# Two more dense groups, a reordered opening and VectorE operands in PSUM in a two-layer graph network kernel on Trainium2

## The reference

```python
edge_index = jnp.stack([src, dst])
deg = jnp.maximum(segment_sum(ones, dst), 1.0); deg_isqrt = deg ** (-0.5)
h = jnp.maximum(_layernorm(x), 0.0)
# layer 0: one of two linear maps per edge, by its type, summed at dst
msg = where(type == 0, h[src] @ W_data.T + b_data, h[src] @ W_control.T + b_control)
x = x + relu(segment_sum(msg, dst) + h @ W_self.T + b_self)
h = jnp.maximum(_layernorm(x), 0.0)
# layer 1: gated sum
g = tanh((h @ gw[:128])[dst] + (h @ gw[128:])[src] + gb)
yn = tanh(ew * yes_w + (1 - ew) * no_w)
e = (g + yn) * 0.5 * deg_isqrt[dst] * deg_isqrt[src]
x = x + segment_sum(h[src] * e[:, None], dst)
```

## Time and profile before

| | us |
|---|---|
| median of 3 runs | 5841.05 (5840.38 to 5857.13) |
| the profiled execution, its own time | 5829.9 |
| its span, first to last instruction | 5828.1 |

### The profile page before, as it was taken

One profiled execution on the slowest core, in us unless ns is written; L12 is line 12 of the kernel. 1 busy time (PEld: TensorE's weight loads), 2 busy tenths in 40 slices (PEclk: granted clock), 3 DMA queues, 4 the chain that ended last, 5 costly groups with the idle time before them and its releaser, 6 DMA issues.

```text
span 5828.1 us, 119944 instructions
## 1 busy us (share of the span) xinstructions
PE 4286.3 (74%) x29542; PEld 3197.4 (55%) x29542; DVE 4365.5 (75%) x16525; ACT 3038.4 (52%) x10494; POOL 4307.3 (74%) x4285
## 2 busy tenths in 40 slices
PE   6588888888888888875577777777777777777754
PEld 5355666655565555553455555555555555555543
DVE  7887777878787777755467777777777777777863
ACT  5666666666666666643254544544445444444530
POOL 5777777777777777777457777777777777777774
PEclk8599999999999999987688888888888888888875
DMA  7777777777777777776355455555555455455544
GB/s 239 245 217 223 222 224 223 225 221 223 225 225 224 223 223 222 220 224 203 102 134 121 118 118 119 121 119 120 119 119 121 119 119 119 118 120 118 120 97 116
DMA packets 764988, 979.91 MB, mean 168 GB/s; under 512 B 135667, under 2 KB 567063, under 8 KB 763799
## 3 DMA queue, kind: packets, MB, share of 16 engines
q1 hardware_dynamic: 620131, 687.26, 40.0%
q0 software_dynamic: 135168, 281.42, 19.7%
q10 hardware_dynamic: 9012, 3.56, 0.2%
HBM read 911.05 MB, written 60.67 MB: 167 GB/s over the span
## 4 chain that ended last, share of the span: by engine, by line
POOL 72%; issue 23%; PE 2%; DVE 2%; DMA 1%; SPq 1%; ACTq 0%; DVEq 0%; POOLq 0%; ACT 0%
POOL G L570 72%; SPq L311 1%; PE PS L883 0%; DMA OWF<-in_x 0%; DMA out<-OWF 0%; DVE ST L1172 0%; DVE OHF L1183 0%; DVE G L1639 0%; PE PS L891 0%; DMA G<-t,IDXB 0%; PE PS L1054 0%; PE PS L1057 0%; DVE OWF L1191 0%; DVE OWF L1832 0%; PE PS L1081 0%
## 5 line engine op out<-in xcount | busy, mean ns | idle before, releaser
L570 POOL DMA_INDIRECT G<-t,IDX x4016 | 4019.1, 1001 | 1274.3 <-issue 1223.0
L1081 PE MATMUL PS<-CDST,HTB 128*128 128x256 f32 x2352 | 868.3, 455 | 447.7 <-DVE CDST L1768 419.9
L705 ACT ACTIVATE OHF<-PS 128x384 bf16<-128x384 f32 x1764 | 864.6, 490 | 515.7 <-PE PS L927 488.0
L939 PE MATMUL PS<-CDST,OHF 128*128 128x256 bf16 x5292 | 901.0, 281 | 35.0 <-DVE ACC L1283 35.0
L797 ACT ACTIVATE ST<-PS,MV 128x1 f32<-128x1 f32 x1764 | 457.5, 259 | 720.2 <-issue 327.6
L1072 PE MATMUL PS<-HTB,OWF 128*128 128x129 f32 x3528 | 815.1, 317 | 9.7 <-DVE OWF L1747 9.7
L1072 PEld LDWEIGHTS PS<-HTB,OWF 128*128 128x128 f32 x3528 | 720.5, 218 | 166.8 <-issue 75.9
L1081 PEld LDWEIGHTS PS<-CDST,HTB 128*128 128x128 f32 x2352 | 408.0, 217 | 556.0 <-ACT HTB L816 510.4
L939 PEld LDWEIGHTS PS<-CDST,OHF 128*128 128x128 bf16 x5292 | 532.6, 101 | 315.8 <-issue 68.7
L1081 PE MATMUL PS<-OHF,OWF 128*128 128x256 f32 x1176 | 438.6, 459 | 246.5 <-DVE OHF L1768 230.2
L1300 DVE TENSOR_SCALAR CDST<-IO,BASE 128x256 bf16<-128x256 int16 x1764 | 510.8, 305 | 5.0 <-PE PS L939 4.1
(11 more groups left out here) (240 smaller groups left out, 8316.9 us busy)
## 6 DMA issues: line engine op xcount, KB each, us to landing
HTB<-t0s SPq DMA_DIRECT2D x442, 384.0 KB
OWF<-t0s SPq DMA_DIRECT2D x440, 384.0 KB
HTB<-t SPq DMA_DIRECT2D x882, 132.0 KB
G<-t,IDX POOLq DMA_INDIRECT x4016
YN<-rows SPq DMA_DIRECT2D x882, 64.0 KB
OHF<-rows SPq DMA_DIRECT2D x882, 64.0 KB
t0s<-HTB SPq DMA_DIRECT2D x25, 384.0 KB
t0s<-OWF SPq DMA_DIRECT2D x24, 384.0 KB
```

Of the source, the lines that this page charges most:

```text
L570: eng.indirect_dma_start(out=G[:, k:k + width], out_offset=None, in_=table, in_offset=bass.IndirectOffsetOnAxis(ap=at, axis=0)).then_inc(s ...
L705: eng.activation(X0[:, k % KX, :, :].rearrange("p n w -> p (n w)"), PS[:, cell_bank(k), 0:384], ACT.Identity).then_inc(q_ev, 1)
L939: ins = eng.matmul(PS[:, 4, 0:DW], X0[:, k % KX, n, :], CD0[:, k % KD, :], start=b == 0 and n == 0, stop=b == NB - 1 and n == 2)
L1081: eng.matmul(PS[:, 4 + g % 2, 0:DW], X1[k % KX1], CD1[k // 2 % 3][:, k % 2, :], start=b == 0, stop=b == NB - 1).then_inc(d_ap, 1)
```

## The change

- RUNS becomes 20 groups of 62 tiles: DT = 1240 dense tiles, 1880 gathers per layer, SM = 235 steps, 1960 cells per layer.
- The opening runs TensorE's `turn` and `messages` in halves of a chunk (4 and 3 blocks), keeps the Relu's result in ACC, forms the self part after all messages, and stores ini after t0. `scales` reads the mean from PSUM (MP). src is loaded before dst, typ earlier; `windows` follows the rows.
- `pair_hots` becomes `quad_hots`: one-hots of four cells (QC) in one operation, with a ring of RT = 6 chunks and three quads. A new tensor NX of 12 KB per partition holds them; dynamic_dma_scratch_size is 4096 for the default.
- The counts OHS are formed by one tensor_reduce in place of two additions.
- In layer 1 the number row IOP and the one-hot OHP lie in PSUM bank 5; the group sum has bank 4 alone; `hot1` and `targets1` move behind `weight1`; target hots are made one pair ahead in five buffers; group_add1 moves into the cell loop.

The diff, cut (TensorE's, ScalarE's and SP's waits follow the renamed semaphores):

```diff
-RUNS = ((16, 62), (2, 60))
+HALF = ((0, 4), (4, CB))
+RUNS = ((20, 62),)
...
-RT = 4
+RU = 4
+RT = 6
+QC = 4
...
-KD1, KX1, KW1 = 6, 6, 8
+KD1, KX1, KW1 = 5, 6, 8
...
+        NX = sb("NX", [128, 3072])
+        HT0 = blocks(ACC[:, 0, 0:NB * 128])
+        MP = PS[:, 2, 0:NB]
+        IOP = PS[:, 5, 0:DW]
+        OHP = PS[:, 5, DW:DW + TG * W].rearrange("p (j w) -> p j w", w=W)
...
             for c in range(NC):
-                if c == 4:
+                if c == 2:
                     eng.wait_ge(s_stg, 1)
                     load(STI, typ, s_typ)
-                eng.wait_ge(a_ye, c + 1)
-                chunk_dma(eng, YB[c % 2], t0, c, False, a_t0[c % 2])
-                if c >= 1:
-                    eng.wait_ge(a_se, c)
-                    eng.dma_start(ini[:, (c - 1) * CB * 128:c * CB * 128],
-                                  ACC[:, 0, (c - 1) * CB * 128:c * CB * 128]).then_inc(s_ini, 16)
...
+                for first, last in HALF:
+                    table_half(c, first, last)
             eng.wait_ge(s_zr, 17)
             for c in (NC - 2, NC - 1):
-                eng.wait_ge(a_t0[c % 2], landed(c, 2))
+                eng.wait_ge(a_t0[c % 2], stored(c))
+            for c in range(NC):
+                eng.wait_ge(a_se, c + 1)
+                eng.dma_start(ini[:, c * CB * 128:(c + 1) * CB * 128],
+                              ACC[:, 0, c * CB * 128:(c + 1) * CB * 128]).then_inc(s_ini, 16)
...
             turn(0)
+            turn(1)
+            for h in range(2 * NC):
+                messages(h)
+                if h + 2 < 2 * NC:
+                    turn(h + 2)
             for c in range(NC):
-                if c + 1 < NC:
-                    turn(c + 1)
...
+                    ins = eng.matmul(PS[:, c % 2 * 2 + n, 0:CB * 64], WS[:, :], ACC[:, 0, at:at + CB * 64],
+                                     start=True, stop=True)
...
                 eng.wait_ge(a_sq, c + 1)
+                eng.tensor_copy(MP[:, cols].unsqueeze(2), MV[:, cols, 0:1])
                 link(eng.reciprocal(RS[:, cols], SQ[:, cols]))
-                eng.scalar_tensor_tensor(DG[:, cols].unsqueeze(2), MV[:, cols, 0:1], -1.0, RS[:, cols].unsqueeze(2),
+                eng.scalar_tensor_tensor(DG[:, cols], MP[:, cols], -1.0, RS[:, cols],
                                          ALU.mult, ALU.mult).then_inc(a_rs, 1)
...
-                eng.wait_ge(m_oh, 2 * n - 1)
-                if n >= 2:
-                    eng.wait_ge(m_os, n - 1)
-                quads = OH[:, b, :, :].rearrange("p (q j) w -> p q j w", j=QT)
-                eng.tensor_tensor(OHT[:, :, :, :], quads[:, :, 0:2, :], quads[:, :, 2:4, :], ALU.add).then_inc(m_oh, 1)
-                eng.wait_ge(m_oh, 2 * n)
-                eng.tensor_tensor(OHS[:, b, :, :], OHT[:, :, 0, :], OHT[:, :, 1, :], ALU.add).then_inc(m_os, 1)
+                eng.wait_ge(m_oh, n)
+                    eng.tensor_reduce(OHS[:, b, :, :], OH[:, b, :, :].rearrange("p (q j) w -> p q w j", j=QT),
+                                      mybir.AxisListType.X, ALU.add).then_inc(m_os, 1)
...
-            def pair_hots(c):
-                eng.wait_ge(q_tc[c % RT], parts_in(c))
-                if c >= 3:
-                    eng.wait_ge(q_ga, HB * (c - 2))
+            def quad_hots(u):
+                for c in (2 * u, 2 * u + 1):
+                    eng.wait_ge(q_tc[c % RT], parts_in(c))
+                if u >= 3:
+                    eng.wait_ge(q_ga, QC * (u - 2))
                 for t in range(2):
-                    ins = eng.tensor_scalar(OT0[c % 3][:, t, :], RB0[:, c % RT, :], PCODE[:, t:t + 1], None,
+                    ins = eng.tensor_scalar(OT0[:, u % 3, t, :], RB0Q[:, u % 3, :], PCODE[:, t:t + 1], None,
                                             ALU.is_equal)
                 ins.then_inc(q_ot, 1)
...
-                        if k % HB == 0 and k + HB < NG * NB:
-                            pair_hots(k // HB + 1)
+                        if k % QC == 0 and k + QC < NG * NB:
+                            quad_hots(k // QC + 1)
...
-                    OH[:, s % 2, :, :], LOC[:, t:t + TG].unsqueeze(2).broadcast_to([128, TG, W]),
-                    IOTA[:, 0:W].unsqueeze(1).broadcast_to([128, TG, W]), ALU.is_equal).then_inc(e_dd, 1)
+                    OHP, LOC[:, t:t + TG].unsqueeze(2).broadcast_to([128, TG, W]),
+                    IOP[:, 0:W].unsqueeze(1).broadcast_to([128, TG, W]), ALU.is_equal).then_inc(e_dd, 1)
...
-                eng.scalar_tensor_tensor(JUNK[k % 2], IO16[:, 0:DW], TABS[:, g % 2, NB + b:NB + b + 1],
+                eng.scalar_tensor_tensor(JUNK[k % 2], IOP, TABS[:, g % 2, NB + b:NB + b + 1],
...
-                if c >= 3:
-                    eng.wait_ge(d_ap, 2 * (c - 2))
-                eng.tensor_tensor(CD1[c % 3], IO16[:, 0:DW].unsqueeze(1).broadcast_to([128, 2, DW]),
+                if c >= KD1:
+                    eng.wait_ge(d_ap, 2 * (c - KD1 + 1))
+                eng.tensor_tensor(CD1[c % KD1], IOP.unsqueeze(1).broadcast_to([128, 2, DW]),
...
+                        if k == (done + 1) * NB + LATE1:
+                            group_add1(done, s - 1)
+                            done += 1
                     if i == 1:
                         score1(s)
-                    if i == 2 and s + 1 < SM:
-                        hot1(s + 1)
-                    if i == 3 and s + 1 < SM:
-                        targets1(s + 1)
                     if i == 4:
                         weight1(s)
+                        if s + 1 < SM:
+                            hot1(s + 1)
+                    if i == 5 and s + 1 < SM:
+                        targets1(s + 1)
```

More of the change, by code:

```diff
@@ L645, in normal, with positive @@
                 ins.then_inc(a_n, 1)
+            def positive(c):
+                for n, (first, last) in enumerate(HALF):
+                    eng.wait_ge(o_t, 2 * c + n + 1)
+                    eng.activation(HT0[:, c * CB + first:c * CB + last, :], strip(0)[:, first:last, :], ACT.Relu)\
+                       .then_inc(o_h, 1)
             eng.wait_ge(s_c, 4)
@@ L650, in _ @@
             normal(0)
-            eng.wait_ge(s_w, 16 * 9)
-            for c in range(NC + 1):
+            root(2, 0)
+            positive(0)
+            normal(1)
+            for c in range(1, NC):
                 if c + 2 < NC:
@@ L1187, in rows @@
             def rows(c):
-                eng.wait_ge(a_m, c + 1)
-                if c >= 2:
-                    eng.wait_ge(a_t0[c % 2], landed(c - 2, 2))
-                eng.tensor_tensor(YB[c % 2], strip(4, 256),
-                                  BB[:, :].unsqueeze(1).broadcast_to([128, CB, 256]), ALU.add)\
-                   .then_inc(a_ye, 1)
+                for n, (first, last) in enumerate(HALF):
+                    eng.wait_ge(o_m, 2 * c + n + 1)
+                    if c >= 2 and n == 0:
+                        eng.wait_ge(a_t0[c % 2], stored(c - 2))
+                    eng.tensor_tensor(YB[c % 2][:, first:last, :], strip(4, 256)[:, first:last, :],
+                                      BB[:, :].unsqueeze(1).broadcast_to([128, last - first, 256]), ALU.add)\
+                       .then_inc(o_y, 1)
             def scales(c):
@@ L1782, in group_add1 @@
                 eng.wait_ge(d_ap, (g + 1) * NB)
[L1783 removed]
+                eng.wait_ge(m_ib, 2 * (SM + NCT + items))
                 if g >= 1:
[L1785 removed]
+                    eng.wait_ge(q_z, NG + g)
                 to = ACC[:, 0, bass.ds(at, DW)]
[L1787 to L1790 removed]
+                eng.tensor_tensor(to, to, PS[:, 4, 0:DW], ALU.add).then_inc(q_z, 1)
+            link(eng.tensor_copy(IOP, IO16[:, 0:DW]))
+            quad_hots1(0)
             for k in range(3):
                 target_score(k)
+            target_hots1(0)
             hot1(0)
@@ L1797, in _ @@
                 ncell = CELL1[s + 1] - CELL1[s]
-                for i in range(max(ncell, 5)):
+                for i in range(max(ncell, 6)):
                     k = CELL1[s] + i
```

287 lines of the change are left out of this document (144 added, 143 removed).

## The result

The changed kernel takes 5397.49 us (median of 4 runs, 5388.35 to 5411.43), the kernel before 5842.56 beside it: a ratio of 0.924, 95% interval 0.922 to 0.926, 445 us less. The forecast was 5400. The lines of the kernel moved: the gathers are L590 (L570 before), the hots of layer 0 L1322 (L1290), TensorE's strips and counts L933 and L939 (L900 and L906), its cells L961 and L973 (L927 and L939), its tiles L992 (L958), the counts L1288 (L1258 and L1260), VectorE's one-hots of the rows, gate and one-hots of the targets in layer 1 L1780, L1794 and L1802 (L1747, L1760 and L1768).

What follows compares the result with a forecast made beforehand. GpSimd's gather after gather was taken as the bound. 97+2413+35+262+2358+22+200 = 5387 us of span, 5389 with the 1.8 outside it, 5400 since the profiled execution lay 11 us below the median; range 5345 to 5560.

Steps and rivals of the forecast that it cites:

- Fewer gathers, same pace in layer 0: Layer 0 main loop: 1880 gathers for 2008 at the old pace of 1.284 us, 2413 us in all.
- A faster gather in layer 1: Layer 1 main loop: operands in PSUM stop VectorE lengthening gathers; pace 1.255 us for 1.328, 2358 us.
- The 22 us for the one bank of the group sum: Layer 1: TensorE waits for group_add1 at 20 groups, a guessed 1 us each, with the edges +22 us.
- Rival D: Layer 1: PSUM operands slow VectorE to 10.7 us a step, 2515 us for 2380, total 5535 us; chance 0.09.
- The terms of VectorE in layer 0: VectorE's need per layer-0 step, from cells, items, tiles and adds: 8.7+1.1 = 9.8 us against GpSimd's 10.27.
- The surcharge of layer 0: Layer 0: 35 us added because GpSimd, VectorE and TensorE are all over 95% taken; nothing given to the six-slot chunk ring.
- engines over 95% taken stall each other in turn: Layer 0 engines: named as what would above all make the forecast fail; no separate size.
- rival E: Layer 0: quad_hots waits for two chunks at once, some 6.0 us a quad, total 6110 us, slower; chance 0.03.
- B: Layer 0: the cells become the bound, 10.9 us a step, +123 for the 35, total 5490 us; chance 0.21.
- the forecast's own signs of being right: Gaps 0.30, gather means 0.95 and 0.98, first gather near 97, GpSimd under 60 us waiting for TensorE, VectorE some 90% busy.
- Opening: Before the first gather: ini stored later, mean read from PSUM; first gather at 97 us, -27.
- Middle and tail: Sections and table between the layers, 262 us, and last sections and output, 200 us: both to stay.

Runs made afterwards that it cites:

- the two runs on the operands: Changed kernel with VectorE's layer-1 operands back in SBUF, 5559.83 us; kernel before with only those operands in PSUM (and what that needs), 5684.39 us.
- the fastest run: Changed kernel with 21 dense groups for 20 and the quad hots of layer 0 made two cells later: 5235.52 us, 0.896 of before.
- the three runs: Changed kernel with hots two cells later, 21 groups and pairs, or pairs and four slots: 8260.97, 8351.38, 8341.87 us where the kernel before took 7871.57.

## Why the prediction was right, point by point

*Fewer gathers, same pace in layer 0.* 1879 intervals at 1.284 were forecast as 2413 us; without the idle places they measure 2412.5.

*A faster gather in layer 1.* Pace 1.255 forecast, 1.261 measured, gather 0.956 for "0.95"; the 0.012 above the 0.944 of an idle VectorE is nearly all L1780, an operation with one tensor input, which the forecast's list of operations with two didn't take in. The cause was argued from one gather of 1.31 us beside L1768 and from the sections' 0.947; the two runs on the operands now show it in both directions, each worth some 160 us. The Trainium skill (SBUF — State Buffer, section "SBUF: two separate sides") says that a VectorE operation with two inputs in SBUF locks the ports that it shares with GpSimd against a GpSimd operation that reads SBUF; the trace agrees (1.048 and 0.956 us with nothing but the operands changed; the gather reads its indices from IDX in SBUF). The 22 us for the one bank of the group sum were too many. From 2900 to 5200 us TensorE's waits show

```profile
PE PS L1116 <- DVE ACC L1821: 82.5, 19, 5.1
```

4.3 us each where I guessed 1, but all hidden: GpSimd waited for nobody.

*Rival D* (PSUM slows VectorE) fell: 0.480 and 0.686 us before and after. The estimate of 0.065 us each from the Trainium skill (VectorE: DVE Perf Modes, section "The TRN2 errata — SBUF-src ops pay a fixed extra latency per instruction") isn't seen at this size, where one of several inputs moved.

*The terms of VectorE in layer 0.* Two hots of four cells take 0.76 us by the forecast, and the timeline shows 0.62 for both:

```profile
1136.73 0.62 DVE L1322 TENSOR_SCALAR NX<-YN,PCODE 128x512 bf16<-128x512 int16 x2 [4.90 <-issue]
```

The count by reduction, 0.598 for 0.490, costs the 0.1 forecast. The need is (2000-208.7)/188 = 9.5 us a step for 9.8; TensorE's busy time 9.6 for 9.8; DMA 247 GB/s and 80% for 252 and 82%.

*The surcharge of layer 0: the step that failed.* 35 us were forecast and 81 came, and the cause was not the one named. I feared for the case that "engines over 95% taken stall each other in turn"; with TensorE busy 96%, in the fastest run, 29 us of waits are left. The wrong sentence is "a quad needs its second chunk five cells after the slot came free, as a pair did; I give it nothing". It counts in cells, and counts one too many, and it takes for granted that what did for 7.6 cells a step does for 9.0: 4 cells are now 4.5 us for 5.4, against loads of 2.9 to 7.1 us, and VectorE and TensorE have less room to catch up. Two cells more, at 21 groups, took away 204 of 233 us of waits. The row above shows a wait of 4.90 us before the quad's hots. This was rival E's mechanism (two chunks at once) at a small dose. With four slots it comes in full: 6475 us where E had said 6110. B's symptoms were there as well (a wait of 1.1 us a step before the hots, GpSimd waiting for TensorE) without B's cause; the first of them is no sign of much, as it was 1.5 before, without harm. Of the forecast's own signs of being right, "under 60 us of GpSimd waiting for TensorE" failed with 101.

*Opening.* 97 forecast, 102.3 measured. The working came to 99 us, and 97 was put down without a reason. The bytes are as worked out, the rate is 246 GB/s for 254:

```profile
DMA packets 27776, 25.08 MB, mean 246 GB/s; under 512 B 1703, under 2 KB 27259, under 8 KB 27387
```

The missing 5 us lie inside the spread of 8 us of this stage over the runs.

*Middle and tail* were to stay and lost 8 and 10 us. The kernel before had, at the starts of the two sections,

```profile
2705.64 0.94 POOL L570 DMA_INDIRECT G<-t,IDXB  x1 [3.45 <-PE PS L906]
...
5636.70 0.94 POOL L570 DMA_INDIRECT G<-t,IDXB  x1 [7.65 <-PE PS L900]
```

where 0.30 stand now. Slot 0 of the five was last used by step 250 of 251, so its first section gather waited for the last step; with 235 steps the last user is 230. In every run with 235 steps (the chip of the three runs aside) the tail's gap is 0.3, in every one with 251 it is 6.9 to 7.7. That is 3.2 and 7.4 us of the 17 (I had not looked at the remainder of steps by slots); the rest of the middle varies by 10 us between runs.

*The sum.* The span came out 22 us above the 5387 worked out (+5 opening, +46 surcharge, -8, -10, -10). That 5400 hits the median of 5397.49 to 3 us is luck in part: the profiled execution of before lay 11 us below its median, that of after 14 above.
